# A four-layer graph network kernel: uneven column chunks (3, 3, 4, 4, 4, 4 tiles), row maxima head by head from masks made in the first sweep, and a regrouped hand-over from the gates to layer 1

## The reference, cut to what matters

```python
# layer 0: A is adj without its diagonal
edge_output = gru(A @ x, x, edge weights)
for each of 3 heads:
    hW = x @ W[head]
    e_plus, e_minus = leaky_relu(scores from (A > 0) @ hW and (A < 0) @ hW)
    att = where(A > 0, e_plus, where(A < 0, e_minus, -9e15))
    edge_support += (softmax(att, axis=1) * A) @ hW / 3
node_output = gru(edge_support, x, node weights)
x = layernorm(x + diag(adj) * (edge_output + node_output))
# layer 1
x = layernorm(x + D^-1/2 adj D^-1/2 @ x @ W.T + b)
```

## Time and profile before

| | us |
|---|---|
| median of 3 runs (lowest to highest) | 2401.54 (2398.70 to 2401.76) |
| the profiled execution, device time | 2404.15 |
| its span in the trace | 2402.4 |
| sweep A, first product to last | 47.8 to 398.1 |
| front phase, to the first product of sweep C | 398.1 to 524.6 |
| sweep C | 524.6 to 1143.0 |
| gates, to the last release of PE | 1143.0 to 1385.8 |
| to the first product of layer 1 | 1385.8 to 1398.5 |
| products of layer 1 | 1398.5 to 1624.9 |
| the rest | 1624.9 to 2402.4 |

### The profile page before, as it was taken

The page is one execution under the profiler, slowest core; times in us unless marked ns, Lnnn a source line. Parts: engine busy times, 40 slices in busy tenths (PEclk is TensorE's granted clock), DMA queues, the critical chain, the costliest instruction groups (busy, mean ns, idle before and its releaser), DMA issues. The chain is left out here.

```text
span 2402.4 us, 25973 instructions
## 1 busy us (share of the span) xinstructions
PE 2132.1 (89%) x9775; PEld 1167.3 (49%) x9784; DVE 1562.4 (65%) x2538; ACT 893.7 (37%) x1273; POOL 93.4 (4%) x131
## 2 busy tenths in 40 slices
PE   6999999659999999999999979997899834999996
PEld 5555556324444444447555434455799822222232
DVE  2454443658696878744678843334788765988987
ACT  2222211458787878756222210001000013434343
POOL 0000000000000000000000010000000002001112
PEclk9999986869999999999999989998899967999998
DMA  5555543445545545456000034540100014323321
GB/s 167 180 193 179 182 150 104 184 138 192 182 166 182 185 164 190 139 189 191 15 1 1 1 92 128 137 115 2 48 18 17 16 45 154 106 78 95 84 79 37
DMA packets 133029, 271.88 MB, mean 113 GB/s; under 512 B 14982, under 2 KB 45544, under 8 KB 129040
## 3 DMA queue, kind: packets, MB, share of 16 engines
q1 hardware_dynamic: 114576, 240.84, 32.0%
q10 hardware_dynamic: 18324, 29.34, 3.2%
HBM read 226.76 MB, written 43.37 MB: 112 GB/s over the span
## 5 line engine op out<-in xcount | busy, mean ns | idle before, releaser
L921 PE MATMUL banks<-arena 128*128 128x512 f32 (+1 forms) x1512 | 587.5, 547 | 36.2 <-DVE arena L1593 34.3
L921 PEld LDWEIGHTS banks<-arena 128*128 128x128 f32 x1512 | 269.2, 191 | 350.9 <-issue 342.1
L1872 DVE SCALAR_TENSOR_TENSOR arena<-arena 128x1024 f32<-128x1024 f32 (+3 forms) x264 | 293.4, 1180 | 27.5 <-PE banks L1050 22.9
L1593 DVE TENSOR_TENSOR arena<-arena 128x1536 f32<-128x1536 f32 (+2 forms) x132 | 202.0, 1530 | 154.6 <-ACT arena L1192 119.5
L828 PE MATMUL banks<-arena 128*128 128x512 f32 (+2 forms) x528 | 247.9, 599 | 0.0
L1041 PE MATMUL banks<-arena 128*64 128x512 f32 (+3 forms) x1056 | 221.3, 559 | 16.1 <-DVE arena L1872 15.9
L1009 PE MATMUL banks<-arena 128*124 128x129 f32 (+2 forms) x1936 | 217.8, 275 | 13.8 <-DVE arena L1790 13.8
L972 PE MATMUL banks<-arena 128*128 128x512 f32 (+2 forms) x528 | 210.1, 551 | 18.2 <-DVE arena L1707 17.1
L1009 PEld LDWEIGHTS banks<-arena 128*124 128x124 f32 (+2 forms) x1936 | 216.1, 187 | 15.6 <-issue 12.8
L1521 DVE CUSTOM_DVE_ANT_0 arena<-arena 128x2708 f32<-128x2708 bf16 (+1 forms) x66 | 196.3, 2974 | 4.4 <-DVE arena L1515 4.4
L1790 DVE SCALAR_TENSOR_TENSOR arena<-arena 128x496 f32<-128x496 f32 (+2 forms) x264 | 167.9, 685 | 42.0 <-PE banks L1009 35.4
(11 more groups left out here) (206 smaller groups left out, 2167.8 us busy)
## 6 DMA issues: line engine op xcount, KB each, us to landing
arena<-adj_T SPq DMA_DIRECT2D x210, 256.0 KB, 3.2
arena<-hw_rows SPq DMA_DIRECT2D x126, 384.0 KB, 3.2
arena<-in_adj SPq DMA_DIRECT2D x21, 1354.0 KB
adj_T<-arena ACTq DMA_DIRECT2D x105, 256.0 KB, 2.0
arena<-in_adj SPq DMA_DIRECT2D x25, 1024.0 KB
arena<-in_adj SPq DMA_DIRECT2D x42, 512.0 KB
hw_rows<-arena SPq DMA_DIRECT2D x21, 384.0 KB, 2.7
arena<-in_adj SPq DMA_DIRECT2D x21, 330.0 KB
```

Of the source, the lines that this page charges most:

```text
L921: ins = PE.matmul(bank(2 * (c % 2) + f)[:, 0:wid(c)], hs[0:R, m % 3, h * D + f * P:h * D + (f + 1) * P], E[0:R, n % 3, h, 0:wid(c)], start ...
L1593: V.tensor_tensor(e, e, a, ALU.mult).then_inc(s["p_ok"], 1)
L1872: V.scalar_tensor_tensor(PM3[0:k, n % 3, h, 0:w], r3_bc[0:k, h, c * WW:c * WW + w], smalls[0:k, 4, h * T + t:h * T + t + 1], mask3[0:k, n ...
```

## The change

- The chunks have 3, 3, 4, 4, 4, 4 tiles: 384, 384, 512, 512, 512 and 404 columns. Every `c * RPC` and `c * W` becomes `FIRST_TILE[c]` and `col(c)`.
- In sweep A the transposes run one unit ahead of the products, not two. While DVE sums the blocks of chunk 0 it also makes the masks of the first three tiles, `mbias_first`; `arow` is used from tile 3 on.
- The front phase has nine row heads, in the order head by head (`place`), and the first needs only the scores of head 0; heads 1 and 2 are waited for at the fourth row head (`e_rest`). `EARLY` is 6, the ring `HWR` has 5 buffers, and the other 16 projected tiles are spread over the nine row heads (`beside`): one or two each. The scores are turned after projected tile 1, not 2.
- Chunk 4 has twelve row heads beside it for chunk 5, not six; the gate weights are loaded at t == 18, not 15.
- In the gates the layer norm of finished tiles comes behind the inputs of the second tanh, `BATCHES` is (0, 8), (8, 15), (15, 22), and the masks of the first four strips of layer 1 are made in the last four tiles. The remaining layer norms alternate with further masks.

```diff
+SIZES = (3, 3, 4, 4, 4, 4)
+CH = len(SIZES)
+FIRST_TILE = [sum(SIZES[:c]) for c in range(CH + 1)]
...
-HWR = 6
-EARLY = 10
-BATCHES = ((0, 11), (11, T - 4), (T - 4, T))
+FIRST = SIZES[0] * H0
+EARLY = 6
+HWR = 5
+BATCHES = ((0, 8), (8, 15), (15, T))
+MASKS_AHEAD = 4
...
+        def place(i, h):
+            return h * SIZES[0] + i if i < SIZES[0] else i * H0 + h
+        def beside(j):
+            return range(EARLY + j * (T - EARLY) // FIRST, EARLY + (j + 1) * (T - EARLY) // FIRST)
...
-            for t in range(3):
-                hw_store(t)
-            sp_rows(sp, "e", e_rows, H0, e_bc)
+            sp_rows(sp, "e", e_rows, H0, None)
+            for h in range(H0):
+                score_load(h)
+                hw_store(2 * h)
+                hw_store(2 * h + 1)
             sp_rows(sp, "d", d_rows, H0, None)
-            for t in range(3, EARLY + 2):
-                hw_store(t)
-            for i in range(1, RPC):
-                row_load(sp, i)
-                for t in range(EARLY - 1 + 3 * i, EARLY + 2 + 3 * i):
-                    hw_store(t)
-            for t in range(EARLY - 1 + 3 * RPC, T):
+            for t in range(2 * H0, T):
                 hw_store(t)
...
-                if c == CH - 2 and t == 15:
+                if c == CH - 2 and t == 18:
...
             transposes_A(0)
-            transposes_A(1)
             for n in range(UNITS):
-                if n + 2 < UNITS:
-                    transposes_A(n + 2)
+                if n + 1 < UNITS:
+                    transposes_A(n + 1)
                 products_A(n)
...
+                if ld.c == 0:
+                    V.tensor_scalar(mbias_first[0:R, :, ld.tiles[0] * R:ld.tiles[0] * R + ld.width], ablk[0:R, ld.buf, 0:SIZES[0], 0:ld.width],
+                                    0.0, NEG, ALU.is_equal, ALU.mult)
...
-                for i in range(RPC):
-                    for h in range(H0):
+                for h in range(H0):
+                    if h == 1:
+                        dve.wait_ge(e_rest, 16 * (H0 - 1))
+                    for i in range(SIZES[0]):
                         row_head(i, h, general)
-                        if EARLY + i * H0 + h < T:
-                            first_part(EARLY + i * H0 + h)
+                        for t in beside(place(i, h)):
+                            first_part(t)
...
-                    for k in normed_at(t, g):
-                        normed_0(k)
+                    if g == 1 and t >= T - MASKS_AHEAD:
+                        masks(t - T + MASKS_AHEAD)
                     dve.wait_ge(g_thok, 2 * t + g + 1)
                     link(V.scalar_tensor_tensor(g_q[0:nr], g_th[0:nr, 0:D], 1.0, g_nh[0:nr, D:2 * D], ALU.add, ALU.mult))
                     V.scalar_tensor_tensor(g_t[0:nr], g_q[0:nr], 0.5, g_nh[0:nr, 0:D], ALU.mult, ALU.add
                                            ).then_inc(g_tok2, 1)
+                    for k in normed_at(t, g):
+                        normed_0(k)
...
+            begun = MASKS_AHEAD
             for k in left_over():
+                masks(begun)
                 normed_0(k)
+                begun += 1
```

More of the change, by code:

```diff
@@ L81, in wid, with col, chunk_of, slot_of @@
 def wid(c):
-    return W if c < CH - 1 else WL
+    return min(N, FIRST_TILE[c + 1] * R) - col(c)
+def col(c):
+    return FIRST_TILE[c] * R
+def chunk_of(t):
+    return max(c for c in range(CH) if FIRST_TILE[c] <= t)
+def slot_of(t):
+    return t - FIRST_TILE[chunk_of(t)]
 def rows_in(c):
-    return [R] * RPC if c < CH - 1 else [R, TAIL]
+    return [kp(t) for t in range(FIRST_TILE[c], FIRST_TILE[c + 1])]
 def blocks2(c):
@@ L240, in build @@
         srow = sb(2, N)
+        first_at = top[0]
         m_bc = sb(2, H0, W)
@@ L531, in sp_rows @@
                 load(sp, bc[:, :, W:N], dram[:, W:N].partition_broadcast(P), rest_bc[k])
-            elif bc is not None:
-                for h in range(heads):
-                    load(sp, bc[:, h, :], dram[h:h + 1, 0:N].partition_broadcast(P).rearrange("p a n -> p (a n)"),
-                         rows[k][4])
         block = ctx.enter_context(nc.Block())
@@ L691, in _ @@
             stage_end(pool, "pool")
-            for i in range(T):
-                pool.wait_ge(b_in, 16 * (i + 1))
+            for i in range(SIZES[0], T):
+                pool.wait_ge(b_in, 16 * (i - SIZES[0] + 1))
                 b = arow[0:kp(i), i * R:i * R + kp(i)]
@@ L986, in _ @@
                 products_1(n)
-                if c and 2 <= t < 2 + RPC:
-                    product_h1((c - 1) * RPC + t - 2)
-            for t in range((CH - 1) * RPC, T):
+                if c and 2 <= t < 2 + tiles_in(c - 1):
+                    product_h1(FIRST_TILE[c - 1] + t - 2)
+            for t in range(FIRST_TILE[CH - 1], T):
                 product_h1(t)
@@ L1137, in _ @@
             node_copy(0)
-            for t in range(3):
+            for t in range(2):
                 node_step(t)
@@ L1143, in _ @@
             act_rows(act, "d", H0)
-            for t in range(3, EARLY):
+            for t in range(2, EARLY):
                 node_step(t)
@@ L1148, in weights @@
             def weights(i, h, general):
-                j = i * H0 + h
+                j = place(i, h)
                 if general:
@@ L1152, in weights @@
                         act.wait_ge(gen_free, j * 4 + q + 1)
+                        if j < FIRST and q == 0:
+                            load(act, arow, adj[i * R:(i + 1) * R, :], gen_in)
                         load(act, d_bc, d_rows[h:h + 1, q * (N // 4):(q + 1) * (N // 4)].partition_broadcast(P).rearrange(
@@ L1178, in distances @@
                 if n < 3:
-                    for q in range(2 * n, 2 * n + 2):
+                    for q in range(max(0, 2 * n - 1), 2 * n + 1):
                         act.wait_ge(hw_out[q], 16 * len(range(q, T, HWR)))
@@ L1507, in _ @@
                 first_part(t)
[L1508 removed]
+            dve.wait_ge(rows["e"][4], 16)
             negative = dve.value_load(has_neg_int[0:1, 0:1])
```

152 lines of the change are left out of this document (79 added, 73 removed).

## The result

The changed kernel takes 2366.53 us (median of 4 runs, 2361.91 to 2367.30) against 2400.12 us before (4 runs, 2390.76 to 2401.76): a ratio of 0.9864, 95% interval 0.9835 to 0.9893. It is 34 us faster where 75 were forecast.

| stage | forecast, us | before | after | measured |
|---|---|---|---|---|
| sweep A, first product to last copy | -50 | 350.4 | 329.7 | -20.7 |
| front phase, to the first product of sweep C | -28 | 126.4 | 102.2 | -24.2 |
| sweep C, to its last copy | +19 | 618.6 | 641.2 | +22.6 |
| from there to the first product of layer 1 | -10.5 | 255.3 | 242.0 | -13.3 |
| products of layer 1, to the last copy | -8 | 226.4 | 220.4 | -6.0 |

The account below looks back on a forecast made before the run. PE, busy 89%, was taken as the bound, with DVE setting the front phase. Terms of -50, -28, +19 and -16 sum to -75 from 2404.15, giving 2329, or 2327 as a median; range 2300 to 2372.

Parts of the forecast that it names:

- the first term: Sweep A: falls from 350.4 to 300 us, a gain of 50, bounds 37 to 58.
- One of 404 columns and 4 tiles 1.35 + 0.21 + 0.47 = 2.03: Sweep A's last chunk: products, mask products and transposes of a unit take 2.03 us.
- A 3.67 us wait becomes about 1.3; I leave 8 us: Sweep A: transposes one unit ahead shorten PE's load wait between chunks; 8 us allowed for five transitions.
- 11 for clock and small waits: Sweep A: 11 us allowed for slow clock and small waits on top of 281 us of units.
- Rival 1: Sweep A's last chunk stays at half clock, 4.06 us a unit, 45 us more, total 2372; chance 10%.
- Rival 4: Sweep A's narrow blocks wait for loads, the ring for stores: 13 + 5 us, total 2345; within the forecast's 70%.
- Front phase: Row heads and projected tiles before sweep C: gain 28 us, bounds 20 to 31.
- The 4.74 us of entry that "stay": Front phase: DVE's idle time on entering the row heads remains 4.74 us.
- Sweep C: Sweep C: an ACT and DVE chain of 19.7 us per narrow group gives a loss of 19 us, bounds 0 to 32.
- rival 2: Sweep C: the chain does not show, narrow chunks run at PE's pace, total 2308; 14% including any better mix.
- Rival 3: Sweep C chunks 0 and 1: PE idles, clock drops to 1.2 GHz, 64 + 69 us more, total 2460; chance 6%.
- Gates and layer 1: Gates through layer 1: 10.5 us from an earlier start, 8 from uniform chunks, 2.5 lost at the end; gain 16, bounds 8 to 20.

Follow-up runs that it names:

- Run 1: Changed kernel with the 20-row piece in sweep A's last chunk transposed and multiplied as a full 128-row piece: 2356.50 us.
- run 5: Changed kernel with the row sums of a block made after its second tile, not its last: 2341.68 us.
- run 2: Changed kernel with sweep A's transposes two units ahead of the products again: 2373.06 us.
- run 6: Changed kernel with the nine row heads beside chunk 0 of sweep C spread apart: 2366.72 us.
- run 7: Changed kernel with the score loads of heads 1 and 2 issued after DVE's entry into the row heads: 2365.22 us.
- run 8: Changed kernel with full-size tail pieces, early row sums, spread heads and late score loads together: 2320.90 us.
- run 9: Changed kernel with full-size tail pieces, early row sums, late score loads and the old chunk sizes 4, 4, 4, 4, 4, 2: 2302.41 us.
- run 13: Kernel before the change with full-size 128-row tail pieces alone: 2375.48 us.
- run 3: Changed kernel with the old chunk sizes 4, 4, 4, 4, 4, 2, all else kept: 2363.29 us.
- run 12: Changed kernel with full-size tail pieces, early row sums, late score loads, and each group's third exponential one unit later in sweep C: 2321.26 us.
- run 11: Kernel before the change with the row sums of a block made after its second tile: 2369.96 us.
- run 14: Chunks of 4, 4, 4, 4, 4, 2 tiles, early row sums and late score loads, with the 20-row pieces put back: 2334.01 us.
- run 4: Changed kernel with chunks of 3, 4, 4, 4, 4, 3 tiles, the last of 276 columns: 2370.82 us.

## Why the prediction was wrong, step by step

**The step that failed** is the first term, "That gives 300 us, a gain of 50", for sweep A; 329.7 us were measured. Its direction and its kinds of loss were right and its size was not: the stated bounds of this part were 37 to 58, and the gain was 20.7. The columns scale as it said (a 384-column unit is 1.81 us, forecast 1.79), and three of its parts are off:

- "One of 404 columns and 4 tiles 1.35 + 0.21 + 0.47 = 2.03": 2.65 us. The parts were taken from a chunk whose pieces are all 128 rows. Run 1 gives 2.04 with pieces of one size. 13.6 us.
- "A 3.67 us wait becomes about 1.3; I leave 8 us": it becomes 2.3, and the waits are 14.3. The release of the block hangs on a row sum that stands on DVE behind ACT's copy and the masks of the last tile; run 5 takes that away and the waits with it. So the block, wanted a unit later, also came free later; that this is why the order brought 1.3 us a transition and not 2.4 (run 2) is inferred. 6.3 us.
- "11 for clock and small waits": 22 units of each chunk at the measured unit times are 296.0 us; with 14.3 of waits, 19.4 are left of the 329.7. Run 5 shows 11 of them to be clock that goes with the waits; the other 8 stay in run 5 (304.9 - 296.0 - 0.6). Most of them lie in chunks 0 and 1, which take 44.9 and 42.3 us there where the units make 39.8, and 2.2 in the very first unit (3.98 us); the cause of the rest is open. 8.4 us.

Together 28.3 of the 29.7 missing us; the last 1.4 are the other units, each a hundredth or two longer than forecast. In the traces of runs 6 and 7 another 5 us are missing, with equal waits and a lower clock. In run 8, with equal pieces and no waits, sweep A is 290.9 us against the 281 of pure units in the prediction.

**The last chunk.** The prediction priced its half clock at the right size and left open what sets it. Rival 1 did not come: PEclk is 1.00. That the measured 2366.5 lies inside the stated 2300 to 2372 is luck all the same, since the range was carried that far for rival 1 alone. Rival 4 did not come either: inside the narrow chunks PE waits 1.2 us for blocks, where it put 13. What the wide chunk gained by its clock it paid partly back in the slow mixed unit, and equal pieces give the narrow chunk its full clock without any new size (runs 9, 13).

**Front phase.** Forecast 28, measured 24.2. Two terms failed. The 4.74 us of entry that "stay" became 7.92, and the first projected tile took 5.16 us and not 2. Against that, the row heads took 49.0 us from entry to the last emptied tile and not 51. Run 7 shows what made the entry longer: with the loads of two heads moved, the DMA engines are 0.64 busy in the stop and not 0.99, and the stop is 3.36 us. The nine heads as such give 3 us (run 3).

**Sweep C.** Forecast +19, measured +22.6; rival 2 falls. The period of a group, 19.97 against 19.7, is the chain; run 12 shortens the chain and the period follows, 19.1. The forecast went no further than the group, and rightly so for its sum, but runs 6 and 12 show that a quicker pace of the heads does not make a shorter chunk. In run 6 the stretch with heads lasts longer; in run 12, 1.7 us come back as PE's wait behind the last head. That wait stands where ACT's logarithm of the denominators follows the last head directly; that this is the cause was read from the timeline and not tried. Rival 3, half clock, came only in small part: PEclk is 0.96 in chunk 0 and 0.95 in chunk 1, where the wide chunk 2 has 1.00, and the chain hides it. Two stretches of chunk 0 in the changed kernel (length, PE busy, PEclk, DMA share, GB/s), the first with waits of 2.35 and 2.55 us at its ends, the second with waits of 0.59:

```profile
504.00:524.00 20.00, 17.41 (x48) 0.91 0.54 192
528.00:533.00 5.00, 4.27 (x13) 1.00 0.38 118
```

The Trainium skill ("TensorE: Matmul & The Clock Gate", section "A second HAM failure mode: psum-queue depth-cycling") says that frequent short idles of PE can make the clock swing between its two levels. In sweep C the two rows agree weakly: 0.91 with the longer waits, 1.00 with the short ones. In sweep A the waits are single ones, but the clock follows them too: a wait of 2.33 us is followed by ten microseconds at 0.50, and without waits (run 5) the same stretch has 1.00. The 148-column chunk with short pieces is not covered by it: in run 11 PE was busy throughout, and the clock was still 0.50.

**Gates and layer 1.** -10.5 and -8 forecast, -13.3 and -6.0 measured; the tail 1.3 against 2.5. Layer 1 starts at once behind the last release, as said (-12.7), but the gates' loop became 0.6 us shorter where 2 us more were forecast.

**The sizes** were meant to bring most of the gain of sweep A, and in sum they give nothing: 15.5 + 3 + 5 us gained, 25.2 lost (run 3). Without the avoidable losses of sweep A they cost 18.5 us by runs 8 and 9, and 18.9 by runs 12 and 9, which shared a chip.

## What to carry to other kernels

Price a new shape by a row of that shape, or bound it from above by the worst mixed row: a short piece between full ones can cost more than the full piece it saves, in time and in clock. When a wait is to shrink because the data is wanted later, also follow what the later order does to the release of the buffer. And before uneven sizes are used to hide a loss, look for the instruction that causes it; here two edits of one or two lines took away what the sizes were to hide, and then the even sizes won.

## What the runs showed of the hardware

- PE at half clock while busy: 148-column units with 20-row pieces ran at 0.50 in all four kernels that have them (before, runs 3, 11 and 14), and the same units with 128-row pieces at 1.00 (runs 9, 13), 49.5 against 21.7 to 24.8 us. At 276 columns the mixed chunk came out either way, 28 us apart (run 4; the clock of the short times is read from their mean). By what way the pieces do it, no row shows.
- Eight short bf16 products took 0.54 us with one 20-row piece in four and 0.21 without; four transpositions 0.65 and 0.47.
- Waits of PE of up to 3.5 us in sweep A went with nearly as much again in clock: 13.7 us of waits and 11 of clock were gone together (run 5 against the changed kernel's trace).
- Where it enters the branch on a value, DVE stood still for 3.36 us with the DMA engines 0.64 busy (run 7), 7.92 with 0.99 (changed), 7.78 with 0.96 (run 3), but 4.74 with 1.02 before: busy DMA engines go with the longer stops, their share alone does not set them. What the engines wait for there, no row shows.
